# Splitting the negated maxima of an attention kernel: three operations on GpSimd in place of two on VectorE

## The reference

```
x = x + xattn(layernorm(x), ctx, mask, mask, Wq, bq, Wk, bk, Wv, bv)
  q, k, v = Wq.t + bq, Wk.s + bk, Wv.s + bv          (256 channels = 16 heads of 16; 512 positions)
  dot  = mask * (q.k / 4) - (1 - mask) * 1e6
  out  = (softmax(dot, axis=-1) * mask) . v
x = x + ffn(layernorm(x))      shared gated layer + router softmax, top 2 of 8 experts, each gated
```

## Time and profile before

| | |
|---|---|
| runs | 688.03, 689.02, 693.57 us; median 689.02 |
| span of the profiled execution | 651.7 us |
| PE busy | 606.6 us, 93% |
| DVE busy | 507.6 us, 78% |
| ACT busy | 472.0 us, 72% |
| POOL busy | 360.0 us, 55% |
| attention (all four engines) | about 48 to 430 us of the span |

### The profile page before, as it was taken

The page is one execution under the profiler, slowest core; times in us unless marked ns, Lnnn a source line. Parts: engine busy times, 40 slices in busy tenths (PEclk is TensorE's granted clock), DMA queues, the critical chain, the costliest instruction groups (busy, mean ns, idle before and its releaser), DMA issues.

```text
span 651.7 us, 12576 instructions
## 1 busy us (share of the span) xinstructions
PE 606.6 (93%) x4110; PEld 259.2 (40%) x4110; DVE 507.6 (78%) x970; ACT 472.0 (72%) x662; POOL 360.0 (55%) x494
## 2 busy tenths in 40 slices
PE   4799999999999999999999999879999999999987
PEld 4543333333333333333333332224554466666532
DVE  2479899999999999999999999964528654454577
ACT  3654899899899899899898888985432276667511
POOL 5559453684684684684684462251553577777310
PEclk9899999999999999999999999999999999999999
DMA  8642434534525535534433432115698533333178
GB/s 293 195 135 76 114 93 145 168 110 144 170 87 168 167 89 171 167 112 146 135 111 102 132 111 80 50 52 121 170 220 184 110 105 106 100 106 107 50 230 310
DMA packets 64990, 88.66 MB, mean 136 GB/s; under 512 B 12624, under 2 KB 45264, under 8 KB 63904
## 3 DMA queue, kind: packets, MB, share of 16 engines
q1 hardware_dynamic: 60032, 68.72, 34.4%
q0 software_dynamic: 4896, 19.14, 12.1%
HBM read 63.75 MB, written 32.74 MB: 148 GB/s over the span
## 4 chain that ended last, share of the span: by engine, by line
PE 76%; DVE 11%; issue 6%; ACT 5%; DMA 1%; POOL 1%; SPq 0%; ACTq 0%; DVEq 0%; POOLq 0%
PE PS L1083 17%; PE PS L986 11%; PE PS L1311 9%; PE PS L1055 8%; PE PS L1774 7%; DVE MX L996 7%; PE PS L845 5%; PE PS L1837 4%; PE PS L1585 4%; ACT E L1069 2%; PE PS L840 2%; PE PS L991 1%; PE PS L933 1%; PE PS L1732 1%; PE PS L929 1%
## 5 line engine op out<-in xcount | busy, mean ns | idle before, releaser
L996 DVE TENSOR_REDUCE MX<-PS 128x1 f32<-128x512 f32 x512 | 323.1, 683 | 17.3 <-PE PS L986 15.4
L1069 ACT ACTIVATE E<-PS 128x1024 f32<-128x1024 f32 x256 | 253.5, 1020 | 32.7 <-PE PS L1055 28.6
L986 PE MATMUL PS<-BIG 53*128 53x512 f16 x512 | 128.6, 384 | 12.2 <-DVE MX L996 10.8
L1083 PE MATMUL PS<-E,BIG 128*32 128x512 f32 x1024 | 136.4, 605 | 2.0 <-ACT E L1069 2.0
L1055 PE MATMUL PS<-BIG 55*128 55x512 f16 x512 | 101.2, 381 | 8.2 <-ACT E L1069 3.5
L879 POOL TENSOR_TENSOR ML<-BIG,ML 128x512 f32<-128x512 f32 x30 | 38.3, 1277 | 102.8 <-ACT BIG L855 102.6
L986 PEld LDWEIGHTS PS<-BIG 53*128 53x128 f16 x512 | 34.3, 93 | 134.0 <-DVE MX L996 120.1
L1796 DVE SCALAR_TENSOR_TENSOR E<-WP,PS 128x352 bf16<-128x352 f32 x39 | 20.3, 521 | 47.0 <-ACT WP L1786 47.0
L1774 PE MATMUL PS<-BIG,CT 128*128 x312 | 53.0, 313 | 1.8 <-DVE WP L1346 1.0
L855 ACT ACTIVATE BIG<-PS,BIG 128x256 f32<-128x256 f32 x64 | 35.7, 560 | 25.9 <-PE PS L840 14.5
L1856 POOL DMA_INDIRECT scr_ys<-SW,bvB x39 | 38.3, 981 | 20.8 <-DVE SW L1849 12.5
(11 more groups left out here) (261 smaller groups left out, 904.0 us busy)
## 6 DMA issues: line engine op xcount, KB each, us to landing
scr_parts<-WP SPq DMA_DIRECT2D x96, 128.0 KB
BIG<-scr_parts SPq DMA_DIRECT2D x64, 192.0 KB
BIG<-in_we POOLq DMA_DIRECT2D x8, 1088.0 KB, 14.1
scr_u<-ML SPq DMA_DIRECT2D x32, 256.0 KB, 3.0
X<-in_x SPq DMA_DIRECT2D x8, 512.0 KB, 6.5
CT<-in_ctx SPq DMA_DIRECT2D x8, 512.0 KB, 4.1
ML<-scr_u SPq DMA_DIRECT2D x16, 256.0 KB
ML<-scr_recs SPq DMA_DIRECT2D x16, 256.0 KB
```

What stands on the lines that cost most here:

```text
L986: e.matmul(PS[:, yi[name] % 3, :], QK[rows, qb(u), 0, j0 + jj, 128 * tt:128 * tt + 128], QK[rows, qb(u), 1, j0 + jj, :], start=True, stop= ...
L996: e.tensor_reduce(MX[:, g % 2, c:c + 1], PS[:, yi[name] % 3, :], AX.X, ALU.max)\
L1069: e.activation(E[:, st, 2 * jj:2 * jj + 2, :], PS[:, slot(name):slot(name) + 2, :], ACT.Exp, scale=1 / 1024).then_inc(s["rc"], 1)
L1083: ins = e.matmul(PS[32 * hh:32 * hh + 32, AVB, :], VT[:, b % 2, st, 4 * (g % 4) + hh, :], E[:, st, hh, :], start=(st == 0), stop=(st == 3))
```

## The change

The split goes from DVE's list to GpSimd's, with the same due time, as three operations: scale in place in MX, copy to half precision, subtract. Between them stand two waits of GpSimd on itself. The first reduction of group g waits, from g = 2 on, until the split of group g - 2 has read MX. The first of GpSimd's three subtractions L804 waits for the sixteenth maximum of group 0 instead of for its split, and since it is due at -.9 and the split of group 0 at -.5736, all three stand ahead of that split on GpSimd.

```diff
@@ split_shared, lower(m), on GpSimd at -.9
                     if m == 0:
-                        e.wait_ge(s["nm"], 1)
+                        e.wait_ge(s["mc"], yi["s", 0, 3, 1, 1] + 1)
@@ scores_max, mx, on VectorE
                             e.wait_ge(s["mp"], yi[name] + 1)
+                            if g >= 2 and tt == jj == a == 0:
+                                e.wait_ge(s["nm"], g - 1)
@@ scores_max, split
-                dch.step(e, e.tensor_scalar(p[:, :, :, 0, :], top, -1 / 32768, None, ALU.mult))
-                e.scalar_tensor_tensor(p[:, :, :, 1, :], top, -1 / 32768, p[:, :, :, 0, :], ALU.mult, ALU.subtract)\
-                    .then_inc(s["nm"], 1)
-            dve.at(when_at[last] + DA + .001 * IT, split)
+                pch.step(e, e.tensor_scalar(MX[:, g % 2, :], MX[:, g % 2, :], -1 / 32768, None, ALU.mult))
+                pch.step(e, e.tensor_copy(p[:, :, :, 0, :], top))
+                e.tensor_tensor(p[:, :, :, 1, :], top, p[:, :, :, 0, :], ALU.subtract).then_inc(s["nm"], 1)
+            pool.at(when_at[last] + DA + .001 * IT, split)
```

## The result

| | before | after |
|---|---|---|
| runs on one chip, median | 688.6 us (4 runs, 688.03 to 693.57) | 699.25 us (4 runs, 696.45 to 699.74) |
| ratio, 95% interval | | 1.0138 [1.0098, 1.0178] |
| profiled execution: span, mean granted clock | 651.7 us, 0.995 | 698.0 us, 0.961 |
| busy: PE, DVE, ACT, POOL | in the table of before | 624.6, 497.5, 472.7, 380.8 us |

The change costs 10.65 us between the medians. The forecast was +4.1 us (693.1 us, at most 697.5 us).

A forecast was written before the change was run, and what follows sets the result against it. PE was taken to set the pace, with DVE's splits covered. Terms of +4.18, -1.78, +2.10 and -.41 summed to +4.09 us, put on the median of 689.02: 693.1 us, range 689.0 to 697.5.

The forecast's parts named there:

- Group 0, the wait: First turn of PE: group 0's split stands behind GpSimd's three L804, so PE waits; +4.18 us (4.07 to 4.28).
- the 1.2 us by a factor of two on all three: Split on GpSimd: alternative estimate with waits, from elementwise work running about twice as slowly there; forecast took .84 us.
- The clock in this wait: Rival, before group 0's turn: TensorE's clock falls in the new wait; at most 3.45 us more, 696.6 us; chance .20.
- The long splits: Groups 1 and 3: DVE no longer held up by GpSimd; PE's waits of 1.03 and .75 us return, -1.78 us.
- The q projection: Once a batch, odd split ahead of k's `split_part` on GpSimd: L845 .42 us late, five times, +2.10 us (0 to 2.60).
- The last groups: From 394.37 us DVE is the bound; group 28's split gives its time back, -.41 us (0 to -.82).
- Steady splits and turns: Groups 4 to 27: splits covered by DVE's idle time, turns by 4.25 us of cover; no change.
- VectorE as the bound everywhere: Rival, throughout the attention: 32 splits of .41 us and the blocked time come back, 678.1 us; chance .10.

The follow-up runs named there:

- the two others with it: Only group 0's split on GpSimd, all others on VectorE, against before: 665.18 us, ratio 1.0127; the changed kernel run again, unchanged: 666.2 us, ratio 1.0156.
- the kernel that put GpSimd only where it has time: Changed kernel with L804 due at -.57, group 0's and odd splits from 5 to 27 back on DVE: 663.24 us, ratio 1.0122 against before.

## Why the prediction was wrong

**Group 0, the wait: right.** 4.11 us were measured (4.11 and 4.11 in the two others with it) against 4.18. The three operations take .27, .20 and .22 us and with their waits .84 (56.64 to 57.48), as forecast; the 1.2 us by a factor of two on all three were too high.

**The clock in this wait: the step that failed, twice.** It stood as a rival with .20. In all three traced executions of a kernel with the idle wait the clock fell. The mean clocks of their other runs say that it falls in those too. My argument against it was that PE is busy without a break on both sides, unlike around 24 us, ahead of the fall in the earlier trace rows. It rested on one fall and on no row of PE idle for 4 us at full rate, and the earlier trace rows show PE idle for 1.03 us at 61.26, so the side behind wasn't without a break. And the price was too low by half. I took the length of the earlier half-rate stretch, 6.9 us, and so 3.45 us at most. Here it lasts 17.1 and 20.5 us, and takes 9.83 - 3.46 = 6.4 and 10.2 - 3.46 = 6.7 us. In group 1 PE is given one dummy per tile; in the one trace where it is given three the stretch is 6.8 us. Also with the right verdict on the clock I would have said 696.6, inside my range; the result was outside it because of the size. With 6.4 for 3.45 this rival gives 689.02 + 4.09 + 6.4 = 699.5; 699.25 was measured. That near is luck in part: the terms of the attention come to 9.58, not 10.5, and the medians are known to some 3 us. The Trainium skill ("TensorE: Matmul & The Clock Gate", Why this matters for your kernels), which warns of idle gaps between bursts of products, pointed to the right case; the trace agrees with 4.11 us.

**The long splits: right.** -.69 and -1.20, together -1.89, against -1.78; the parts were -1.03 and -.75. In group 1 less came back, since PE's next product then waits .35 us for the reduction anyway. Group 3 gave .45 more than PE's idle time there. The idle time of a row was the wrong measure: from one L986 to the next PE took 1.13 us in before (89.01 to 90.14), while with the splits on GpSimd both start at 88.80, and the projection behind them (L929) starts 1.4 us earlier (89.34 in place of 90.74), of which .21 are from ahead. What GpSimd was in there was L879, a multiplication, not a subtraction.

**The q projection: right in place and mechanism, half in size.** L845 is .41 us late, forecast .42, but the reductions behind it only .22 to .23: +1.12 in place of +2.10. Shown by the kernels with the odd splits on DVE, in which the steps are gone. The step that erred is the one that passed PE's lateness on whole.

**The last groups:** -.18 in place of -.41, within its bounds. **Steady splits and turns:** nothing, as said; the shift is flat there.

**The bound:** VectorE as the bound everywhere is refuted by the flat shifts (it would have been a fall of .41 in each group), and the split doubled in even groups shows the cover from the other side.

In sum, with 4.14 for the wait and 9.83 - 3.46 = 6.37 for the clock, the small terms are 9.58 - 4.14 - 6.37 = -.93 where I had -.09, and the clock +6.4 where my sum had none.

**Open.** What exactly lowers the clock: it also fell once without any idle time over 1 us. What sets how long the half rate lasts: with one dummy per tile it was 10.2 to 23.9 us. The half rate at 430 to 439 us in two executions and between 631 and 652 us in six, and ACT's pauses in the expert stage.

## What to carry to other kernels

A small step moved to another engine costs not its duration but its place in that engine's list: look up what stands ahead of it at each of its occurrences, the first above all, where set-up work is still queued. If TensorE has to idle there, don't price the half rate that may follow by an earlier stretch of another density: here it lasted 6.8 us in one place and up to 24 us in another; and if a wait can't be avoided, dummy products through all of it bought back two thirds of the loss here (groups 0 to 2: 3.46 in place of 9.83 us). An operation can be split by occurrence: here the same three instructions gained where DVE would have stood still behind GpSimd (groups 1 and 3) or set the pace (the last groups), and lost where GpSimd's list fed the next product.

## What the runs showed of the hardware

**An instruction of DVE can stand still for the whole of one of GpSimd.** Small operations of .17 us on DVE lasted 1.04, 1.22, 1.23, 1.26 and 2.84 us, each time until .03 us after the end of the multiplication or subtraction that GpSimd was in (L879, L882 or L804), in both forms used here; the reductions, which read PSUM, took .65 to .69 us in every trace, beside any work of GpSimd. The Trainium skill ("SBUF — State Buffer", Who interferes with whom) says that an instruction of DVE with two inputs in SBUF, or in a two-port mode, and one of GpSimd that reads SBUF exclude each other for a whole instruction, and that a reduction doesn't take part; the traces agree. A split on DVE is thus as dear as the instruction of GpSimd that it meets.

**Half rate followed idle times of 1.57, 2.11, 2.37 and 4.11 us**, and lasted from 6.8 to 24 us (50.3 to 74.2 in the kernel that put GpSimd only where it has time), while PE was busy in the records at 1.2 GHz for nearly all of it that lay behind the wait. The 1.03 us of before at 61.26 were not followed by it, and one fall (53.7 us) came without such an idle time.

**Operations of 128x16 on GpSimd** cost .20 (copy to half precision), .22 (subtraction) and .26 us (scaling), 1.1 to 1.5 times the .17 us of DVE.
